# Attention and routed feed-forward on one core: half-width masks, last output tiles multiplied ahead, and steps moved within the engines' orders

## What is computed

```python
# x: (4, 1024, 256) float32; 16 heads of 64; 32 experts, 8 tokens each, hidden 1024
xn  = layernorm(x)
q, k, v = split_heads(xn @ Wq), split_heads(xn @ Wk), split_heads(xn @ Wv)
q, k = apply_rope(q), apply_rope(k)
sim  = where(causal, einsum('bid,bjd->bij', q, k) * 64**-0.5, -inf)
attn = merge_heads(softmax(sim) @ v) @ Wo + bo
# feed-forward: softmax over the tokens of the gate's logits, top 8 tokens of each expert,
# their weighted sum is merged, goes through gelu(m @ w1 + b1) @ w2 + b2, and is
# scattered back to the tokens with the same weights
out  = x + attn + ffn(xn)
```

## Time and profile before

| | |
|---|---|
| three timed runs | 1415.09, 1419.10, 1420.23 us; median 1419.1 us |
| the profiled execution | 1423.84 us |
| its span in the trace | 1422.0 us |
| mean granted clock of TensorE | 0.984 |
| TensorE busy | 1350.8 us, 95% |
| GpSimd, VectorE, ScalarE busy | 974.1, 897.5, 631.3 us |
| DMA | 189.78 MB, mean 133 GB/s |

### The profile page before, as it was taken

The page is one execution under the profiler, slowest core; times in us unless marked ns, Lnnn a source line. Parts: engine busy times, 40 slices in busy tenths (PEclk is TensorE's granted clock), DMA queues, the critical chain, the costliest instruction groups (busy, mean ns, idle before and its releaser), DMA issues.

```text
span 1422.0 us, 31224 instructions
## 1 busy us (share of the span) xinstructions
PE 1350.8 (95%) x11556; PEld 880.9 (62%) x11556; DVE 897.5 (63%) x1186; ACT 631.3 (44%) x954; POOL 974.1 (68%) x662
## 2 busy tenths in 40 slices
PE   6799999989899999999999999999999999999989
PEld 5465666655556555556676776666666776666647
DVE  5778777845666566666346766666667666666631
ACT  3355565542444445434324444454444444444430
POOL 2566677755665676566566776888789768888861
PEclk9799999999999999999999999999999999999999
DMA  5314233575678667864641321212232222212111
GB/s 175 113 68 157 93 118 135 183 247 193 224 272 282 226 208 246 274 231 159 180 153 54 94 79 57 80 65 76 86 107 91 68 81 93 76 62 76 46 50 60
DMA packets 123712, 189.78 MB, mean 133 GB/s; under 512 B 29680, under 2 KB 58768, under 8 KB 123568
## 3 DMA queue, kind: packets, MB, share of 16 engines
q1 hardware_dynamic: 93136, 113.42, 23.8%
q10 hardware_dynamic: 30384, 74.23, 15.4%
q0 software_dynamic: 48, 0.13, 0.1%
HBM read 131.63 MB, written 22.54 MB: 108 GB/s over the span
## 4 chain that ended last, share of the span: by engine, by line
PE 83%; DMA 5%; ACT 4%; DVE 3%; issue 3%; SPq 1%; POOL 0%; ACTq 0%; POOLq 0%; DVEq 0%
PE t_pO L1410 17%; PE t_pF L1385 12%; PE t_pA L1308 9%; PE t_pF L1368 7%; PE t_pB L1308 6%; PE t_pA L1332 3%; PE t_pC L1332 3%; PE t_pA L1313 2%; PE t_pC L1419 2%; PE t_pB L1313 2%; PE t_pB L1470 2%; DMA t_swap<-t_raw 2%; PE t_pC L1470 2%; PE t_pB L1460 2%; PE t_pC L1460 2%
## 5 line engine op out<-in xcount | busy, mean ns | idle before, releaser
L701 POOL TENSOR_TENSOR t_acc<-t_acc,t_PT 128x1024 f32<-128x1024 f32 (+3 forms) x256 | 438.9, 1715 | 168.7 <-ACT t_PT L772 149.4
L1410 PE MATMUL t_pO<-t_PT,t_V 128*64 128x512 f32 (+3 forms) x1536 | 293.2, 503 | 9.4 <-issue 5.0
L676 POOL TENSOR_TENSOR t_swap<-t_swap,t_sin 128x512 f32<-128x512 f32 x124 | 164.7, 1329 | 194.5 <-DMA t_swap<-t_raw 194.5
L772 ACT ACTIVATE t_PT<-t_pA 128x1024 f32<-128x1024 f32 x192 | 169.7, 884 | 270.1 <-PE t_pA L1320 233.0
L1385 PE MATMUL t_pF<-t_xT,t_wqk 128*128 128x512 f32 x756 | 212.5, 417 | 5.5 <-issue 3.8
L1410 PEld LDWEIGHTS t_pO<-t_PT,t_V 128*64 128x64 f32 x1536 | 94.4, 137 | 149.3 <-issue 127.2
L679 POOL TENSOR_TENSOR t_rot<-t_rot,t_swap 128x512 f32<-128x512 f32 x124 | 178.0, 1436 | 9.8 <-POOL t_swap L676 0.2
L1385 PEld LDWEIGHTS t_pF<-t_xT,t_wqk 128*128 128x128 f32 x756 | 134.4, 191 | 46.7 <-issue 14.1
L1036 DVE TENSOR_TENSOR t_LO<-t_rot,t_HI 128x512 fp32r<-128x512 f32 x124 | 156.0, 1258 | 7.5 <-ACT t_HI L804 7.5
L794 ACT ACTIVATE t_raw<-t_pF 128x512 f32<-128x512 f32 x124 | 74.0, 597 | 169.1 <-PE t_pF L1385 147.1
L772 ACT ACTIVATE t_PT<-t_pB 128x768 f32<-128x768 f32 (+1 forms) x192 | 142.0, 739 | 13.4 <-PE t_pB L1320 11.1
(11 more groups left out here) (206 smaller groups left out, 2417.8 us busy)
## 6 DMA issues: line engine op xcount, KB each, us to landing
t_w1t<-in_L_ffn_w ACTq DMA_DIRECT2D x32, 1024.0 KB, 5.9
t_w2t<-in_L_ffn_w ACTq DMA_DIRECT2D x32, 1024.0 KB, 8.7
t_swap<-t_raw SPq DMA_DIRECT2D x248, 128.0 KB, 2.1
t_OT<-r_s SPq DMA_DIRECT2D x128, 128.0 KB, 2.9
t_wqk<-wqk_s SPq DMA_DIRECT2D x24, 512.0 KB, 3.4
xt_s<-t_xs SPq DMA_DIRECT2D x6, 1024.0 KB, 5.2
t_xT<-xt_s ACTq DMA_DIRECT2D x6, 1024.0 KB, 6.4
t_wvs<-wv_s SPq DMA_DIRECT2D x12, 512.0 KB, 3.8
```

The source lines that it names most:

```text
L676: pool.tensor_tensor(swap_of(r), swap_of(r), sin[:, c * BANK:(c + 1) * BANK], ALU.mult).then_inc(sin_sem, 1)
L701: pool.tensor_tensor(a[:, :, off:], a[:, :, off:], pt, ALU.add).then_inc(acc_done, 1)
L772: act.activation(PT[:, n % PTS, :, 0:w], bank[:, :, 0:w], ACT.Exp, scale=SCALE).then_inc(exp_done, 1)
L1410: mm = pe.matmul(pO[h * DH:(h + 1) * DH, off:], v, PT[:, n % PTS, h, 0:w], start=(j == 0), stop=(j == 4 * c + 3))
```

## The change

1. **Masks by halves.** `maskq` is a 64x64 identity per head. The diagonal block of 128 columns is written as two halves of 64: still four multiplications per block, each of 64 columns where it had 128, with a stationary operand of 128 columns as before. `maximum` now has the table (`maskd`) as stationary operand.
2. **Last output tiles ahead.** For batch 3, `part(t)` multiplies seven of the eight pairs (three fp32r multiplications each) and the feed-forward part. Parts 0 to 4 stand in stages 1 to 5 of pair 31, part 5 in stage 1 and parts 6 and 7 in stage 2 of "pair" 32. VectorE adds x and bias and keeps the tile in `yp` (`keep`). The last pair is one fp32 multiplication per tile (`last`), which VectorE adds (`finish`). Two tiles are stored together. `round_part` and `rest_of_part` split `OT` for it on ScalarE and VectorE. `Wo` isn't loaded a second time; one block of it is (`wlast`).
3. **First exponentials early.** ScalarE loads the Exp table ahead and runs the first two exponentials of pair 0 before `high` of ("q", 0, 1) and ("k", 0, 1). Statistics of batches 1 to 3 and their roots come some stages later.
4. **VectorE's order.** `invert` stands after `rope` in its stage, `normalise` at the end of its stage (in "pair" 32 where it was). In SyncE's list `store_recip` comes after the swap's DMAs and `load_sums`.
5. **TensorE's order.** In stage 2 of pairs 6 to 13 `fill` stands between the two `maximum` calls. The first tile of batch 0 comes after `values`.

```diff
-        tiles = [(), (0, 1), (2,), (3,), (4, 5), (6, 7)][g]
+        tiles = {2: (0, 1, 2, 3), 3: (4, 5, 6, 7)}.get(g, ())
...
+PARTS_AT = {(N - 1, 1): [0], (N - 1, 2): [1], (N - 1, 3): [2], (N - 1, 4): [3], (N - 1, 5): [4], (N, 1): [5], (N, 2): [6, 7]}
...
-STATISTICS_AT = {(0, 1): (2, 0), (0, 3): (2, 1), (0, 4): (3, 0), (0, 5): (3, 1)}
+STATISTICS_AT = {(0, 2): [(1, 0)], (0, 3): [(1, 1)], (0, 4): [(2, 0)], (0, 5): [(2, 1), (3, 0)], (1, 0): [(3, 1)]}
...
+        def shifted(mask, d, r):
+            return mask[d, (1 - r) * DH:(1 - r) * DH + P128]
...
@@ SyncE
-                n2 = normalise_of(*STAGES[s - 2]) if s >= 2 else None
-                if n2 is not None:
-                    store_recip(n2)
                 f = fill_of(P, g)
...
                 if n is not None:
                     load_sums(n)
                 if n2 is not None:
+                    store_recip(n2)
                     spread_recip(n2)
...
@@ ScalarE
+            def round_part(t):
+                act.wait_ge(o_done, 2 * (N - 2) + t // 4 + 1)
...
+                act.activation(oh[:, t % 2, 0:PAIRS - 1, :], OT[:, 0:PAIRS - 1, t * P128:(t + 1) * P128], ACT.Copy).then_inc(oh_done, 1)
...
+            act.activation(nmax[:, :], one[:, 0:1], ACT.Exp)
+            weights_high(("qk", 1))
+            exp(0, 0, 0)
+            high(("q", 0, 1))
+            exp(0, 0, 1)
+            high(("k", 0, 1))
...
@@ VectorE
+            def keep(t):
+                dve.wait_ge(y_part, t + 1)
+                dve.wait_ge(xb_done, (B - 1) * NT + t + 1)
+                dve.tensor_tensor(yp[:, t, :], out_bank(t), xb[:, t % 2, :], ALU.add).then_inc(y_kept, 1)
+            def finish(t):
+                dve.wait_ge(y_mm, (B - 1) * NT + t + 1)
+                dve.wait_ge(y_kept, NT)
+                dve.tensor_tensor(yp[:, t, :], out_bank(t), yp[:, t, :], ALU.add).then_inc(y_done, 1)
...
             for s, (P, g) in enumerate(STAGES):
-                n = normalise_of(*STAGES[s - 2]) if s >= 2 else None
-                if n is not None:
-                    invert(n)
                 pair, banks = maxima_of(P, g)
...
                     rope(fill_of(P, g))
+                n = normalise_of(*STAGES[s - 2]) if s >= 2 else None
+                if n is not None:
+                    invert(n)
                 n = normalise_of(*STAGES[s - 3]) if s >= 3 else None
-                if n is not None:
+                if n is not None and P == N:
                     normalise(n)
...
+                for t in next_parts(s):
+                    rest_of_part(t)
+                n = normalise_of(*STAGES[s - 3]) if s >= 3 else None
+                if n is not None and P < N:
+                    normalise(n)
...
@@ TensorE
-                            mm = pe.matmul(bank[:, h, 0:P128], maskk[d, r, :], maskq[d, r, :], start=False, stop=(r == 1))
+                            mm = pe.matmul(bank[:, h, half], shifted(maskk, d, r), maskq[d, :], start=False, stop=(r == 1))
...
-                                mm = pe.matmul(bank[:, h, at + w - P128:at + w], maskq[d, r, :], maskk[d, r, :],
-                                               start=False, stop=(r == 1))
+                                mm = pe.matmul(bank[:, h, half], shifted(maskd, d, r), maskq[d, :], start=False, stop=(r == 1))
...
+            def part(t):
+                bank = out_bank(t)
+                if t >= 2:
+                    pe.wait_ge(y_kept, t - 1)
+                else:
+                    pe.wait_ge(y_done, (B - 1) * NT)
+                pe.wait_ge(ol_done, (B - 2) * NT + t + 1)
...
+            def last(t):
+                pe.wait_ge(y_kept, NT)
+                if t >= 2:
+                    pe.wait_ge(y_done, (B - 1) * NT + t - 1)
...
+                    if m == 1 and after_gelu and fill_of(P, g):
+                        fill(fill_of(P, g))
...
-                if fill_of(P, g):
+                if fill_of(P, g) and not after_gelu:
                     fill(fill_of(P, g))
...
+                for t in parts_of(P, g):
+                    part(t)
                 for y, t in outputs_of(P, g):
-                    output(y, t)
+                    if y == B - 1:
+                        last(t)
+                    elif not first_tile:
+                        output(y, t)
...
                 for chunk in chunks:
                     values(*chunk)
+                if first_tile:
+                    output(0, 0)
```

More of the change, by code:

```diff
@@ L250, in attend_block @@
         hT = sb("t_hT", [P128, 2, P128])
+        with nc.sbuf_tensor("t_yp", [P128, NT, C], F32) as yp, nc.sbuf_tensor("t_wlast", [P128, C], F32) as wlast:
+            pass
         xT = sb("t_xT", [P128, 2, 2, KT, BANK], F32R)
@@ L405, in next_outputs, with next_parts, parts_before @@
             return outputs_of(*STAGES[s + 1]) if s + 1 < len(STAGES) else []
+        def next_parts(s):
+            return parts_of(*STAGES[s + 1]) if s + 1 < len(STAGES) else []
+        def parts_before(s):
+            return sum(len(parts_of(*t)) for t in STAGES[:s])
         def fill_bank(f):
@@ L706, in input_and_bias @@
                 pool.wait_ge(x_loaded[t % 2], (n // 2 + 1) * 16)
-                if n >= 2:
+                if y == B - 1 and t >= 2:
+                    pool.wait_ge(y_kept, t - 1)
+                elif n >= 2:
                     pool.wait_ge(y_done, n - 1)
@@ L750, in _ @@
                 for y, t in outputs_of(P, g):
-                    input_and_bias(y, t)
+                    if y < B - 1:
+                        input_and_bias(y, t)
+                for t in parts_of(P, g):
+                    input_and_bias(B - 1, t)
         @block.scalar
@@ L937, in _ @@
                     copy_sums(normalise_of(*STAGES[s - 1]))
-                for chunk in chunks[after_gelu:]:
+                for chunk in chunks[after_gelu:] if s else []:
                     exp(*chunk)
@@ L1276, in _ @@
                     weigh()
+                for t in parts_of(P, g):
+                    keep(t)
                 for y, t in outputs_of(P, g):
-                    output(y, t)
+                    if y < B - 1:
+                        output(y, t)
+                    else:
+                        finish(t)
                 for x_ in slots_of(P, g):
```

113 lines of the change are left out of this document (74 added, 39 removed).

## The result

The changed kernel takes 1412.1 us (median of 12 runs; the kernel before took 1420.95 us beside them), a ratio of 0.9938 with a 95% interval of 0.9913 to 0.9963. That is 8.8 us or 0.6% faster, where 41 us were forecast, and 1412.1 lies outside the range. Its profiled execution took 1406.38 us (17.5 us under the profiled one of before), span 1404.6 us, mean granted clock 0.986.

What follows compares the result with a forecast made beforehand. TensorE, busy for 95% of the span, was taken as the bound. Masks 13.6, stage 2 11.7, division 5.6, first tile 1.0, start 2.4 and clock 6.8 sum to 41.1 us: median 1419.1 to 1378 us, range 1360 to 1398.

Steps and rivals of the forecast that it cites:

- Masks: TensorE's masks, in every stage: halving their columns saves 0.028 us in each of 512 groups, 13.6 us in all.
- The first rival: The masks gain nothing, because the second pair of multiplications waits for its weights: 1392 us, chance 25%.
- Stage 2 after a Gelu: Pairs 6 to 13: TensorE's waits before the second bank of maxima and the turned slots shrink, 11.7 us.
- VectorE's division at the stage's end: Slot reads now come before the division, saving TensorE 5.6 us; nothing counted for holding up the next stage's maxima.
- What I said would prove me wrong: Sign in the changed kernel's timeline: `t_nm` or `t_nma` appear among the releasers of TensorE.
- the last rival: Slower: reciprocals stored behind the swap make all 64 divisions late, ahead of the maxima, 60 us: 1438 us, chance 3%.
- Clock: Three stretches at clock 0.50 after TensorE's waits go, in full or by half: 6.8 us saved.
- Start: TensorE's wait for the first exponential ends near 40.0 instead of 42.40: 2.4 us saved.
- the statistics: Statistics moved off VectorE's early stages are beside other work; nothing was counted for them.
- First output tile: Of TensorE's 3.0 us wait for a DMA of the first output tile, 1 us is saved.
- Last tiles: Kernel's end: TensorE's saving is taken back by handing over between engines, 0 counted, ends 6 us less or more.
- a sign of being wrong: Sign at the kernel's end: the last sums wait for `t_OT`.

Runs made afterwards that it cites:

- masks_only: The kernel before with only the masks changed to 64-column halves: 1407.3 us, ratio 0.9919.
- light_masks: before_light with the new masks alone: the masks are worth 14.7 us there.
- before_light: The kernel before, with expert weights after the first two experts fetched only as a 128x128 piece each: 1402.7 us, ratio 0.9882.
- after_light: The changed kernel, with expert weights after the first two experts fetched only as a 128x128 piece each: 1387.9 us, ratio 0.9771.
- start_undone: The changed kernel with the start of the kernel before (first exponentials behind the weights' rounding, statistics at their old stages): 1407.0 us, ratio 0.9921.
- all_three: later_early with both the start and the last output tiles of the kernel before: 1386.2 us, ratio 0.9778.
- values_early: The changed kernel with the value weights (512 KB) fetched one stage earlier: 1411.5 us, ratio 0.9957.
- later_early: The changed kernel with each division one stage later and the value weights fetched one stage earlier: 1392.1 us, ratio 0.9815.
- combined: later_early with the last batch's output tiles as in the kernel before: 1396.1 us, ratio 0.9842.

## Why the prediction was wrong

**Masks: right.** 13.6 us forecast, 13.2 (`masks_only`) and 14.7 (`light_masks` against `before_light`) measured. In the timeline of the changed kernel around one mask, beside the earlier trace rows, the second scores step comes 384.21 - 383.88 = 0.33 us after the mask's start, as forecast:

```profile
383.88 0.23 PE L1400 MATMUL t_pA<-t_maskq,t_maskk 64*128 64x64 bf16 x4
383.95 0.42 PE L1388 MATMUL t_pB<-t_HI 64*128 64x384 f32 x2
...
384.21 0.34 PE L1388 MATMUL t_pB<-t_LO,t_HI 64*128 64x384 f32 x2
```

Over the groups of the scores the second pair of a mask's multiplications started 67 ns after the first in the median, and starts 39 ns after it now: the 0.028 us of the prediction. The first rival, that the second pair waits for its weights, falls. The estimate from the Trainium skill (TensorE: Matmul & The Clock Gate, Weight-path perf modes) gave a saving of 0. It took 53 ns for a load where the trace of before has 94 in the median; the measurement decides.

**Stage 2 after a Gelu: right in its stage, lost in the sum.** Forecast 11.7 us over eight stages; the trace has 11.0 over the seven of pairs 7 to 13. But less than half is left without the megabytes. In the light kernels stage 2 gains 66.7 - 62.3 = 4.4 us. The other 6.6 go with the transfers: VectorE's reciprocal for `t_comp` starts 3.6 to 6.4 us into stage 2 in `before` and 3.6 to 4.3 us into it in `before_light`. Moving the step that waits for them didn't buy this part: the wait turned up at the division.

**The step that failed** is in "VectorE's division at the stage's end": that the division "now holds up the next stage's maxima where its DMA is late", "Nothing is counted for that", with the cover that "the bank of maxima is read about a microsecond into a stage, and TensorE has scores and a projection ahead". The cover was too short. In the timeline above TensorE begins the first bank at 384.80 and is done with the second bank and the projection at 389.22 - 1.83 = 387.39; VectorE is let go only at 387.30 and then has the division and 1.22 us of maxima to do. Measured price: 17.4 us in eight waits (2.2 each), with the clock 19.8 us over stage 0 of seven pairs. That is most of the 41.1 - 17.5 = 23.6 us by which the profiled executions miss the forecast. The 5.6 us for it did come (the waits for `t_g` and `t_part` in the earlier trace rows are down to 0.3 us). What I said would prove me wrong is there too: `t_nma` and `t_nmb` among TensorE's releasers. The mechanism is that of the last rival, to which I gave 3%; its place was right and its count wrong: 8 divisions, not 64, those of pairs 5 to 12, which have both the megabytes beside them and a slot behind them. Three more late divisions, of pairs 22, 25 and 30, hold `values` for 4.7 us in all (`PE t_pO L1490 <- issue: 4.7, 3, 2.3`), and that of pair 22 does so in `after_light` too (2.6 us), so not every one of these waits needs the megabytes.

**Behind it stands a second error**: the earlier trace rows show VectorE waiting 2.48 and 4.36 us for DMAs of 4 and 128 KB, and I took these lengths as given. The view of DMA transfers of before would have told more. Over the whole span, and then in 350 to 640 us alone:

```profile
t_swap<-t_raw SPq DMA_DIRECT2D x248, 128.0 KB, 2.1
t_OT<-r_s SPq DMA_DIRECT2D x128, 128.0 KB, 2.9
```

```profile
t_swap<-t_raw SPq DMA_DIRECT2D x52, 128.0 KB, 5.4
t_OT<-r_s SPq DMA_DIRECT2D x24, 128.0 KB, 4.5
```

The same transfers take 3.3 and 1.6 us longer where the weights stream in, just where my two terms lay.

**Clock: 6.8 us forecast, 3.1 came** (lost time is span x (1 - clock): 22.8 us before, 19.7 after). The stretches of 301 and 325 us in the earlier trace rows are gone, that of the start has stayed, and new ones come with the new waits. (I read them as beginning after a wait. Those at 41.72 and 301.13 begin inside it, since the waits end at 42.40 and 303.1.) With the waits of 2.9 us from 338.9 on and of 3.3 us from 620.0 on, the windows view of the changed kernel has:

```profile
342.10:345.50 3.40, 3.40 (x22) 1.07 (x15) 3.40 (x4) 0.60 (x1) 2.99 (x3) 0.51 1.05 390
...
622.00:628.80 6.80, 5.50 (x30) 1.66 (x32) 4.29 (x7) 0.46 (x1) 6.64 (x6) 0.50 0.48 152
```

**Start: 2.4 us forecast, none found.** The wait itself went as forecast: 3.21 us until 42.40 became 0.42 us until 39.70. But a wait of 0.89 us follows at 41.71, and TensorE waits 2.67 us for `t_nma` until 80.62, the line shown above. VectorE is at the moved statistics from 71.68 to 78.51 us, ahead of those maxima. "I count nothing" for the statistics was thus a second term put at nothing: all twelve traces with the new start have such a wait (0.9 to 2.9 us) at 77 to 86 us, and none of the eight with the old one. The changed kernel has pair 1 start 4 us early, but so have `start_undone` and `before_light` with the old start (89.9 and 90.4 us). Over the kernels of both kinds that start lies between 89.9 and 96.6 us: 6.8 to 15.4 us are lost at the lower clock ahead of it, which moves it by more than the edit.

**First output tile:** its DMA wait went from 3.0 to 1.9 us, the 1 us forecast. **Last tiles: 0 forecast, about 2 us lost, within its ends.** From the end of the last `values` to the last addition it is 20.6 us, with 20 forecast, and the waits are those for `t_ol` ahead of parts 6 and 7 (2.2 and 1.6) and for `t_OT` among the sums (1.2), the last of which I had named as a sign of being wrong. Pair 31 to the end takes 65.1 to 67.0 us in the traces with parts and 64.5 to 65.9 in those with the new masks and the old tail. With what each lost at the lower clock there taken off, the two sets stand apart: 64.4 to 65.4 us with parts, 62.5 to 63.3 without.

**The sum.** With the megabytes gone, the change is worth 14.8 us (`before_light` to `after_light`), where the forecast terms come to 41.1. Masks (14.7) and stage 2 (4.4, of which the masks have none: `light_masks` takes 66.9 us there) account for all of it; 2.4 us are lost at the end (63.1 to 65.5). The kernel before loses 17 us by itself when the megabytes go (`before_light`), most of it in pairs 5 to 13, and this waiting was what much of the rest of the forecast was to remove. The forecast's 1378 us wasn't out of reach (`all_three`, 1386), but needed the waiting steps behind the maxima and not merely elsewhere.

**Left open:** why the masks alone add 6.4 us of waiting in pairs 7 to 13, which the lower clock then makes longer, when a fixed landing time would leave the pairs as they were. That the transfers fall worse against each other when stages shorten is only argued; the median landings differ too little to show it.

## What to carry to other kernels

When a wait goes, ask whether its releaser was an engine or a transfer: an engine's wait can be filled, a late transfer only moves the wait to the next step in line. Count where each moved step stands against *every* reader behind it on its in-order engine, and put the step that waits for a DMA behind all that others wait for, a whole stage late if its result isn't needed sooner. Measure an edit again once a larger wait is out of its way: fetching the value weights early was worth nothing on one kernel and 11 us on the next. Steps moved "beside other work" have a place in an in-order list too: look at what stands behind them.

## What the runs showed of the hardware

Transfers of 128 KB on one queue take 1.6 to 3.4 us longer beside megabytes on another, at a mean DMA share of only 0.68 to 0.69. Those of 4 KB take 1.6 to 1.8 us longer in the order of the changed kernel, and no longer in that of before (2.0 and 1.4 us with the megabytes, 1.9 and 1.9 without). Executions of one kernel lie up to some 20 us apart (1404.5 to 1424.4 us for `values_early`), and differences of that size can be the clock: the profiled executions of `later_early` (clock 0.993) and `combined` (0.981) differ by 17.2 us, and time lost at the lower clock differs by 26.7 - 9.7 = 17.0 us. Halving the moving columns of a small bf16 multiplication from 128 to 64, with the stationary operand as wide as before, saved 0.03 us in each group of four: the group's second pair starts 39 ns after the first instead of 67.
